# Layer-0 attention: the value matmuls of a query tile as one block instead of four quarters

## The reference, cut to what matters

```python
final_logits = pi[0] * logits[:, None, :, :] + score     # (b, h, n, m), score = q k / sqrt(8)
attn = jax.nn.softmax(final_logits, axis=-1)
out = jnp.einsum('bhnm,bhmd->bhnd', attn, v)
```

## Time and profile before

| | us |
|---|---|
| time before, median of 3 runs | 1829.59 |
| lowest and highest run | 1827.02, 1834.72 |
| the profiled execution's own time | 1839.94 |
| its span, first to last instruction | 1838.2 |
| `attend_quads`, first batch, from the first transposes to the last row matmuls | 91.7 to 367.9 |
| the same, second batch | 435.9 to 709 |
| PE busy in the span | 1478.4 (80%) |
| DVE, ACT, POOL busy | 1027.7, 859.8, 697.0 |
| mean granted clock of TensorE | 0.886 of full speed |

### The profile page before, as it was taken

The page is one execution under the profiler, slowest core; times in us unless marked ns, Lnnn a source line. Parts: engine busy times, 40 slices in busy tenths (PEclk is TensorE's granted clock), DMA queues, the critical chain, the costliest instruction groups (busy, mean ns, idle before and its releaser), DMA issues. The chain is left out here.

```text
span 1838.2 us, 42125 instructions
## 1 busy us (share of the span) xinstructions
PE 1478.4 (80%) x15527; PEld 978.1 (53%) x15527; DVE 1027.7 (56%) x2775; ACT 859.8 (47%) x1544; POOL 697.0 (38%) x1372
## 2 busy tenths in 40 slices
PE   3799999968999995327994269999997699999935
PEld 2476666655666674315763145555555355555524
DVE  5656555484655655570231765666665566666553
ACT  2355455544554552000221146677764377767622
POOL 1266556524665661015355023333332234333300
PEclk9999999989999998558997567999997589999968
DMA  4000000000000000521343016676660367766400
GB/s 124 1 1 2 3 1 2 2 1 1 1 2 2 2 1 1 170 102 65 65 94 64 5 56 195 189 205 197 201 190 16 107 196 208 210 195 193 140 1 23
DMA packets 104953, 148.74 MB, mean 81 GB/s; under 512 B 13750, under 2 KB 61238, under 8 KB 104758
## 3 DMA queue, kind: packets, MB, share of 16 engines
q1 hardware_dynamic: 97974, 141.22, 26.0%
q0 software_dynamic: 6784, 4.87, 2.0%
HBM read 68.49 MB, written 77.21 MB: 79 GB/s over the span
## 5 line engine op out<-in xcount | busy, mean ns | idle before, releaser
L658 DVE CUSTOM_DVE_ANT_0 t_Z<-t_psS,a0b_L 128x1024 f32<-128x1024 f32 x256 | 311.1, 1220 | 185.4 <-issue 182.7
L716 ACT ACTIVATE t_Pt<-t_psT 128x512 f32<-128x512 f32 x512 | 278.6, 595 | 252.9 <-PE t_psT L614 252.9
L1001 ACT ACTIVATE t_Pt<-t_psT 128x512 f32<-128x512 f32 x512 | 285.5, 595 | 146.4 <-PE t_psT L819 86.9
L904 DVE TENSOR_REDUCE t_mm<-t_psS 128x1 f32<-128x640 f32 (+1 forms) x256 | 219.6, 858 | 221.6 <-DMA t_A<-relative_rows 160.2
L614 PE MATMUL t_psT<-idf,t_Z 128*128 128x128 f32 x2048 | 285.1, 283 | 8.3 <-POOL t_Z L681 4.7
L681 POOL TENSOR_SCALAR t_Z<-t_Z,t_m 128x1024 f32<-128x1024 f32 x256 | 287.3, 1122 | 0.0
L614 PEld LDWEIGHTS t_psT<-idf,t_Z 128*128 128x128 f32 x2048 | 225.9, 144 | 59.5 <-issue 32.1
L805 PE MATMUL t_psS<-a1b_KT,a1b_QT 72*128 72x384 bf16 (+3 forms) x864 | 224.5, 313 | 10.7 <-DVE t_mm L905 10.4
L991 ACT ACTIVATE t_rows<-t_psT 128x512 f32<-128x512 f32 x256 | 153.2, 599 | 49.4 <-PE t_psT L797 43.1
L845 PE MATMUL t_psO<-t_Pt,t_Vh 128*32 128x128 f32 x4096 | 170.3, 286 | 6.6 <-DVE t_Os L928 6.6
L588 PE MATMUL t_psO<-t_Pt,t_Vh 128*32 128x128 f32 x4096 | 164.6, 280 | 0.3 <-ACT t_Pt L716 0.3
(11 more groups left out here) (260 smaller groups left out, 1817.5 us busy)
## 6 DMA issues: line engine op xcount, KB each, us to landing
relative_rows<-t_rows SPq DMA_DIRECT2D x256, 256.0 KB, 3.0
t_A<-relative_rows SPq DMA_DIRECT2D x192, 192.0 KB, 3.4
t_A<-relative_rows SPq DMA_DIRECT2D x64, 128.0 KB, 2.8
x_B<-in_b SPq DMA_DIRECT2D x1, 4096.0 KB, 18.7
x_A<-in_a SPq DMA_DIRECT2D x1, 4096.0 KB, 27.0
a1b_QT<-t_mr SPq DMA_DIRECT2D x192, 1.0 KB
expert_rows<-zp SPq DMA_DIRECT2D x1, 2740.0 KB, 13.1
x_xe<-expert_rows SPq DMA_DIRECT2D x8, 342.5 KB, 3.0
```

The lines of the kernel that those rows point to most:

```text
L658: nc.vector.tensor_tensor_reduce(out=Z[:, j, :], in0=psS[:, j % 2, :], in1=L[:, qt, :], scale=1.0, scalar=3e38, op0=ALU.add, op1=ALU.min, ...
L716: nc.scalar.activation(Pt[:, qt % 2, j, half * (N // 2):(half + 1) * (N // 2)], psT[:, half, :], ACT.Exp).then_inc(s_exp, 1)
L904: v.reduce_max(mm[:, u % AR, 1:2], psS[:, u % 2, width:N], AX)
L1001: nc.scalar.activation(Pt[:, q % PR, :], psT[:, unit_item(G, i) % RR, :], ACT.Exp).then_inc(s_exp, 1)
```

## The change

`values` loses its argument `part` and the test around its waits; it runs all 8 key tiles at once. In `quad` it is called at j = 1 alone, after T and S of that item, in place of a quarter at each j. The order of the 64 matmul instructions among themselves, their operands and their waits are the same, and the `s_pv` increment stands behind the last of them as before. After the last quad the last query tile's values, which already were four quarters in a row, are one call.

```diff
-                def values(hq, qt, part, first):
+                def values(hq, qt, first):
                     g = hq * QT_N + qt
-                    if part == 0:
-
-                        pe.wait_ge(s_exp, (g + 1) * J * 2)
-                        if qt == 0:
-
-                            pe.wait_ge(s_vh, hq + 1)
-                        if qt == GRP or (qt == 0 and not first):
-
-                            pe.wait_ge(s_os, hq * 2 + qt // GRP)
-                    for kt in (2 * part, 2 * part + 1):
+
+                    pe.wait_ge(s_exp, (g + 1) * J * 2)
+                    if qt == 0:
+
+                        pe.wait_ge(s_vh, hq + 1)
+                    if qt == GRP or (qt == 0 and not first):
+
+                        pe.wait_ge(s_os, hq * 2 + qt // GRP)
+                    for kt in range(QT_N):
                         for j in range(J):
                             last = nc.tensor.matmul(psO[32 * j:32 * j + 32, (qt % GRP) * P:(qt % GRP + 1) * P], Vh[:, kt, j, :],
                                                     Pt[:, qt % 2, j, kt * P:(kt + 1) * P], start=kt == 0, stop=kt == QT_N - 1)
-                    if part == 3:
-                        last.then_inc(s_pv, 1)
+                    last.then_inc(s_pv, 1)
...
-                        if qt:
-                            values(hq, qt - 1, j, first)
-                        elif not first:
-                            values(hq - 1, QT_N - 1, j, False)
+                        if j == 1 and qt:
+                            values(hq, qt - 1, first)
+                        elif j == 1 and not first:
+                            values(hq - 1, QT_N - 1, False)
...
-                for part in range(J):
-                    values(QUADS - 1, QT_N - 1, part, False)
+                values(QUADS - 1, QT_N - 1, False)
```

## The result

| | before | changed |
|---|---|---|
| median, first comparison | 1828.38 us (4 runs, 1827.02 to 1834.72) | 1810.79 us (4 runs, 1806.55 to 1815.89) |
| median, second comparison | 1842.98 us (11 runs, 1835.37 to 1852.92) | 1815.3 us (6 runs, 1809.77 to 1824.89) |
| ratio, first and second | | 0.9869 (0.9832 to 0.9906), 0.9843 (0.9812 to 0.9874) |
| profiled execution, span | 1838.2 us | 1814.2 us |
| first T to last T of the two batches | 270.1 and 267.2 us | 257.7 and 256.8 us |

The account below looks back on a forecast made before the run. PE was taken to set the pace, with no DMA mattering. Per batch -16.3 + 0.5 + 3.8 + 0.3 = -11.7 us, for two -23.4, from the median 1829.6 to 1806 us; range about 1797 to 1819.

Parts of the forecast that it names:

- One: Items without V (T and S only): 1.405 us against 2.03 before, 1.43 for the first behind a block of V.
- Two: The item that holds all of V: 3.34 us against 2.03, as three more quarters cost 1.30.
- the ring: PE and ACT over half of psT: T to exp 0.66, exp 0.60, then 0.14 to next T, together 1.40 us.
- Three: Three items from T behind V to the next V item: the chain's 4.21 us fits their 4.24, costing nothing.
- the chain: T to S 0.90, S to Z 0.64, Z to sub 1.49, sub 1.12, 0.06 until T: 4.21 us.
- Four: At qt 5 and qt 1, DVE's wait for F delays Z; PE stands 0.55 us, 7 times a batch: 3.8 us.
- Five: Waits that move, chiefly around ACT's copy of psO, with the exp behind it late: +0.3 us net a batch.
- Six: Ends of a batch: the last V block stands in items without scores, +0.5 us; the tail is unchanged.
- A: PE alone sets items without V, at 1.34 us, so more is gained: 1793 us; chance 0.08.
- B: Chain from S to T falls behind, nearly all of 0.54 us a query tile lost: about 1825 to 1830; chance 0.07.
- C: Clock falls to half in items without V, 1.16 us more each; 1862 with one tile in four; chance 0.05.

Follow-up runs that it names:

- the eight blocks: Kernel before the change, each quarter of V cut in two, one key tile before S and one behind it in every item: 1893.98 us, ratio 1.0267.
- the wide ones: Kernel before the change, each four narrow V matmuls made one with 128 weight columns, values of three heads left out: 1769.42 us, ratio 0.9612.

## Why the prediction was right, step by step

**One and Two held.** The V item was forecast at 3.34 and took 3.31 to 3.34 (3.37 in the tiles behind F); the items without V at 1.43 and 1.405 took 1.43 and 1.41 outside the loop and 1.36 and 1.39 inside it. The cause of 1.40 was the ring, as stated: with a shorter exp it went to 1.31. That a block costs 0.24 to 0.29 in addition to its matmuls is shown by the eight blocks, and that this comes with the narrow weights by the wide ones.

**Three was mis-sized inside the loop.** There the chain is 4.31 and not 4.21: T to S takes 0.93 behind a V block (I had the 0.90 of an item without one), and from the end of sub to T it takes 0.14 and not the 0.06 of the earlier trace rows. The text said that it had no cover and would come out one for one, and it did: the fourth item takes 1.55 in the loop, and the tile 7.64. Outside the loop the chain is about 4.23 and fits in, as forecast: the last quad has 7.57. The 7.62 of the first quad comes from the late exp of j = 0, which I did not have. The 7 tiles of the first quad, 16 of the loop and 7 of the last give 7 x 0.505 + 16 x 0.48 + 7 x 0.555 = 15.1 us in a batch, where 16.3 were forecast.

**Four held, in mechanism and nearly in size.** Z was to start 4.97 after T and did so 4.94 after it in the first quad and 5.09 in the loop; PE stood 0.67 for it there. An event costs 0.58 in the first quad (1.958 + 1.493 in place of 1.407 + 1.466), 0.62 to 0.65 in the loop and 0.68 to 0.71 in the last quad, 4.5 us for the seven of a batch against 3.8. What I did not have was the rule behind it, which my own expectation for V at j = 0 showed by failing.

**Five was too high.** The item in which ACT copies psO takes what its neighbours take in the first quad and in the loop, and 0.06 more in the last quad; the 0.3 that it cost before is gone. That is 0.1 less in a batch, where +0.3 was forecast.

**Six held:** the four last items cost 0.50 more.

**The sum, and luck in it.** The sum of these sizes is -15.1 + 0.5 + 4.5 - 0.1 = -10.2 for a batch, or 20.4 us for two, not 23.4. Measured were -12.5 and -10.4 in the trace of the result, and -12.4 and -7.9 in the second trace. The terms were off by 1.2 and 0.7 us one way and by 0.4 the other; that the first trace gave 22.9 all the same is luck. It lies in the stretches at half clock: there the first batch's start took 1.1 less than before and the second's 1.3 more, and the two turns 1.5 and 1.7 less; in the second trace the second turn took 1.8 more than before.

**The rivals.** A does not hold outside the loop while the exp is 0.60. Inside the loop it is partly so: the ring does close faster there, and the first two items take 1.36 and 1.39, but the chain takes it back in the third, as the text against A had it. B was right on the place inside the loop; of its 0.5 us a tile some 0.06 came. C did not happen: the clock in the windows is the same.

## What to carry to other kernels

Where matmuls with narrow weights stand between wide ones, count the blocks and not the matmuls: here each block cost 0.24 to 0.29 us. Its length didn't matter: with 1.31 for T and S and 0.109 for each batch of four, a quarter leaves 2.03 - 1.31 - 0.44 = 0.28 and the whole leaves 3.31 - 1.31 - 1.74 = 0.26. Fewer blocks paid until the items without one ran into the next ring, here psT and the exp. A long block is also cover: put it between a step that holds another engine and the instruction that needs that engine's next result, and place it by the distance between those two, not by how early the first can start.

## What the runs showed of the hardware that I had not expected

From the end of an exp to the T that waits for it, PE took 0.07 us in the quads inside the loop (175.94 + 0.60 to 176.61) and 0.14 outside it (99.39 + 0.60 to 100.13), for the same wait; items that this ring sets are 0.07 shorter in the loop. From the end of a sub to the T that waits for it, it goes the other way: 0.13 to 0.14 in the loop (169.26 + 1.12 to 170.51) and 0.06 outside it. Why was not tried. A chain timed in straight code is therefore not that of a loop.

PE stood idle 3.0 to 3.5 us where the loop over quads turns back, before the change and in every kernel with the whole V at j = 1, and 2.1 to 2.4 with V at j = 2, in both kernels tried; with V at j = 0 it was 2.9 and 3.2, in eight blocks it was 2.8, in two blocks 3.2 and 4.0, and with wide weights nothing. Behind such a wait the granted clock was at half for several us in most cases, but it stayed full once behind 3.01 and twice behind 2.2 to 2.3, and fell behind 2.06: the length of the wait alone does not tell.
